# First layer of a two-layer decoder: some units of its hand-written pipeline in other slots

## The chip, the cores and the metric

The kernel runs on one core of a Trainium2 chip. Its time is the device time of one execution in microseconds (us), lower is better, given as the median of three runs. TensorE (PE) multiplies and transposes, VectorE (DVE) and ScalarE (ACT) work elementwise, GpSimd (POOL) works elementwise and issues indirect DMAs, SyncE (SP) issues the plain DMAs.

## The reference

`x` is 16 sequences of 256 tokens with 256 features. Each of two layers adds three branches to it, each on a layer norm of the running `x`:

- Layer 0: causal linear attention with 16 heads (features elu+1); cross attention with 16 heads of 16 to a context of 77 rows; a mixture of 16 experts, of which each token takes two. A token's place with its expert is a running count over all tokens before it (`ranks = cumsum(onehot)`), and a place beyond the capacity of 640 drops the token.
- Layer 1: attention over a latent, cross attention to the same context, and a gated feed-forward with quantised weights.

All arithmetic is float32.

## The kernel before, in words

`layer0` does the two attentions of layer 0 and the router, for 8 groups of 512 tokens (4 tiles of 128). `experts` then runs the 16 experts over the slots, `layer1` and the feed-forward follow. Each of these is a block that ends in a barrier over all engines.

In `layer0` the order of each engine's work is written out by hand. A loop variable `t` counts slots; `g, s = t // 8, t % 8` is a group and one of its 8 steps (lines 297 to 301). In step s of group g the engines work on several groups at once: the linear attention of group g, the preparations of groups g+1 and g+2, the output of g-1, the cross attention of g-2 and g-3, and the router of g-4. `back1` means that group g-1 exists, `ahead1` that g+1 does. From g = 8 on no new linear attention starts and the pipeline drains; the last slot is in g = 12. Engines are told apart by their own copies of the loop (SP from line 406, POOL 526, PE 785, ACT 982, DVE 1231), and each executes its list strictly in order.

PE works into eight banks. Four hold scores (L570 the linear attention's, L585 the cross attention's) and are refilled when DVE has copied them out (L1081, L1093). The other four are handed out in turn to "units", in the order of the table `UNITS` (lines 312 to 319): a unit's `room` waits until the unit four places earlier has been copied out of the same bank by ACT or DVE. So the order in the table says who waits for whom, also where no data are passed.

The units and steps that matter here:

- `turn0`, `turn1`, `turn2`: transposes of the three normalised inputs (L615). `turn1` (of g-1) feeds the queries of the cross attention, `turn0` (of g+2) the linear attention's projections.
- `proj0` (L670): the first half of the linear attention's output projection; DVE adds the residual (L1130) and so frees its bank. The residual with its bias is made by POOL (L516).
- `state0`, `state1` (L649): sums of keys times values for the next group; DVE copies them (L1156).
- `xk` (L679): the context's keys, of g-1. ACT repeats the tail of the context (`repeat_tail`, L944), then copies the keys twice (`keep_x_keys`, L935).
- `xt..` (L705, L710): transposes of the cross attention's probabilities. A tile's way to them is: scores (PE L585), mask and maximum (DVE L1093, L1097), 16 exponentials (ACT L959), sum and reciprocal (DVE L1102, L1104), product with the reciprocal (POOL L508, L509, in `normalised`), transposes (PE).
- The router: `logits`, `gate`, then `choose` on DVE (top two experts, one-hot matrix M, L1173 to L1190), `rank` (PE L774, L777), `count_ranks` (DVE L1197 to L1202), `place_tokens` (DVE L1207 to L1213), `scatter` (POOL, two times four indirect DMAs, L524), `weigh` (DVE L1219 to L1229), and two small stores of places and weights by SP (L448, L449).
- `moments`, `deviation`, `shifts`: a layer norm's statistics on DVE, the reciprocal root on POOL (L488), the shift on DVE (L1146); ACT then normalises (L979).
- `context_unit` (L141, L151, L160): work for layer 1, put into the slots of the drain.

After the last slot SP waits for all scatters and for one of the context units (`xv4`), loads the first expert's slots (L1376), and waits for its stores. SP's own order puts the stores of the last group's places and weights ahead of that load:

```
if k == 1 and there(g - 5):
    s.wait_ge(q.slots_ready, g - 4)
    ...                                   # two stores (L448, L449)
...
s.wait_ge(scattered, 16 * TOPK * NT * NG)
wait_later_made(s, "xv", 4)
load_first_slots(s, c, dr)
s.wait_ge(q.x2_stored, 16 * NG)
s.wait_ge(q.stored, 32 * NG)
```

Of the kernel before, what the change touches and what calls it, by code (L numbers as in the profile page):

```python
# [23 lines left out]
NG = B * S // T  # L24
# [153 lines left out]
def layer0(nc, ctx, c, io, dr):  # L178

    st = ExitStack()  # L180
    with st:
# [114 lines left out]

        FIRST, LAST = -2 * NS + 2, (NG + 4) * NS + 2
        WARM = 44
# [10 lines left out]
        def turned(j):  # L309
            return tuple(f"xt{j}_{n}" for n in range(NTURN))  # L310

        UNITS = {0: (("k0", 1), ("k1", 1), ("tok2", -1), ("tok3", -1), ("xq1", -2), ("xval0", -3)),
                 1: (("val0", 0),) + tuple((n, -3) for n in turned(2)) + (("col1", -1), ("xk", -1), ("v0", 1)),
                 2: (("xproj0", -3), ("proj1", -1), ("pkt", 1)),
                 3: (("val1", 0),) + tuple((n, -3) for n in turned(3)) + (("turn2a", -4), ("turn2b", -4), ("v1", 1)),
                 4: (("tok0", 0), ("tok1", 0), ("q0", 1), ("q1", 1), ("xval1", -3), ("logits", -4)),
                 5: (("val2", 0),) + tuple((n, -2) for n in turned(0)) + (("col0", 0), ("xproj1", -3), ("gate", -4)),
                 6: (("proj0", 0), ("turn1a", -1), ("turn1b", -1), ("turn0a", 2), ("turn0b", 2),
                     ("rank", -4), ("state0", 1), ("state1", 1)),
                 7: (("val3", 0),) + tuple((n, -2) for n in turned(1)) + (("xq0", -1), ("xvm", -1), ("xvl", -1))}  # L320
        place, used, front, turn_of = {}, [0, 0, 0, 0], {}, 0
# [61 lines left out]
        with nc.Block(no_gpsimd_drain=True) as block:  # L383
# [74 lines left out]
            def _(g_):  # L458
# [69 lines left out]
                for t in range(FIRST, LAST):  # L528
                    g, s = group_step(t)
                    if s == 3 and there(g + 2):  # L530
                        deviation(0, g + 2)
                        if g + 2 == 0:
                            clear_rooms()
                    if s == 1 and there(g - 3):
                        normalised(g - 3, 3)
                    if s % 2 and s > 1 and there(g - 2):
                        normalised(g - 2, s // 2 - 1)
                    if s in (0, 1) and there(g - 5):
                        scatter(g - 5, s)
                    if s == 2 and there(g + 1):  # L540
                        one_of_two(g + 1)
                    if s == 4 and there(g - 1):
                        deviation(1, g - 1)
                    if s == 5 and there(g):
                        add_bias(g)
                    if s == 7 and there(g - 3):
                        deviation(2, g - 3)
# [3 lines left out]
            def _(p):  # L551
# [230 lines left out]
                for t in range(FIRST, LAST):  # L782
# [26 lines left out]
                    if s == 1:  # L809
                        if back3:  # L810
                            x_turn(g - 3, 2)
                        if back1:
                            wait_kept(p, "tok2", g - 1)
                            wait_kept(p, "tok3", g - 1)
                            to_columns("col1", g - 1, at, 1)
                        if back1:
                            x_keys(g - 1)
                        if ahead1:
# [10 lines left out]
                    if s == 3:  # L829
                        if back3:  # L830
                            x_turn(g - 3, 3)
                        if back4:
                            turn_norm(2, g - 4, h2[(g - 4) % 2])
                        if ahead1:
                            v_rows(g + 1, 1)
                    if s == 4:
                        if now:
# [11 lines left out]
                    if s == 5:  # L849
# [9 lines left out]
                        if back4:  # L859
                            gate(g - 4)  # L860
                    if s == 6:
                        if now:
                            wait_kept(p, "col0", g)
                            project("proj0", g, aT, wo, 0)
                        if back1:
                            turn_norm(1, g - 1, h1)
                        if ahead2:
                            turn_norm(0, g + 2, h0)
                        if back4:
                            ranks(g - 4)  # L870
                        if ahead1:
                            states(g + 1, 0)
                            states(g + 1, 1)
                    if s == 7:
# [6 lines left out]
                        if back1:  # L881
                            x_rows_v(g - 1)
                    for name, j in later_at(t):
                        context_unit(name, j)
# [3 lines left out]
            def _(a):  # L888
# [92 lines left out]
                for t in range(FIRST, LAST):  # L981
# [19 lines left out]
                    if s == 1:  # L1001
                        if back3:
                            by_key(g - 3, 2)
                        if back1:
                            keep_columns("col1", g - 1, aT, 1)
                            repeat_tail(g - 1)
                            keep_x_keys(g - 1)
                        if ahead1:
# [4 lines left out]
                    if s == 3:  # L1013
# [4 lines left out]
                        if ahead1:  # L1018
                            keep_v(g + 1, 1)
                    if s == 4:  # L1020
                        if ahead2:
# [38 lines left out]
            def _(v):  # L1060
# [170 lines left out]
                for t in range(FIRST, LAST):  # L1231
# [9 lines left out]
                    if s % 2 and s > 1 and back2:  # L1241
                        sums(g - 2, s // 2 - 1)
                    if s == 1 and there(g - 5):
                        weigh(g - 5)
# [41 lines left out]
                    if s == 6:  # L1286
# [3 lines left out]
                        if back3:  # L1290
                            wait_kept(v, "xproj0", g - 3)
                            wait_kept(v, "xproj1", g - 3)
                            moments(2, g - 3, x2)
                        if back4:
                            count_ranks(g - 4)
                        if ahead1:
                            keep_state(g + 1, 0)
                            keep_state(g + 1, 1)
                    if s == 7:
                        if back1:  # L1300
                            keep_x_tail(g - 1)
                        if back3:
                            shifts(2, g - 3)
                        if back4:
                            place_tokens(g - 4)
                    for name, j in later_at(t):
                        if name == "vo":
# [1721 lines left out]
```

## Time and profile before

| | us |
|---|---|
| runs | 1669.12, 1663.44, 1670.83; median 1669.12 |
| profiled execution, its own time | 1666.73 |
| its span in the trace | 1664.7 |
| PE busy | 1514.0 (91%) |
| DVE busy | 1014.5 (61%) |
| ACT busy | 900.2 (54%) |
| POOL busy | 473.1 (28%) |

The first layer's pipeline takes the first 596 us of the span, the experts go on to about 900. In the trace a group of 8 steps takes 57 to 62 us while the pipeline is full: step 0 of g = 4 begins at 209.9, of g = 5 at 271.2, of g = 6 at 332.8. Then g = 8 begins at 446, g = 9 at 487, g = 10 at 524, and the drain ends at 591.

A timeline row reads: start, duration, engine, line, operation, out<-in, shape, count; in brackets the idle time of the engine just before it and what ended it. A duration over several instructions (x4) is from the first's start to the last's end.

### The profile page before, as it was taken

How to read it: one execution, taken by the hardware profiler on the slowest of the kernel's cores; microseconds unless marked ns; L12 is line 12 of the kernel's file. 1: busy time of each engine (PE TensorE's matmuls, PEld its weight loads, DVE VectorE, ACT ScalarE, POOL GpSimd, SP SyncE). 2: the span in 40 equal slices, each digit the busy share in tenths (PEclk: the TensorE clock that was granted, in tenths of full speed). 3: DMA queues.
4: the chain of work that ended last, by engine and by line, in shares of the span. 5: the costliest groups of instructions: out<-in, count | busy, mean ns of one | idle time of the engine just before them, and what ended most of it. 6: DMA issues, size and time to landing. Idle time of an engine off the chain costs nothing. (4 is left out here: it accounts for less than half of the span.)

```text
span 1664.7 us, 26844 instructions
## 1 busy us (share of the span) xinstructions
PE 1514.0 (91%) x9735; PEld 1071.9 (64%) x9735; DVE 1014.5 (61%) x2312; ACT 900.2 (54%) x2289; POOL 473.1 (28%) x625
## 2 busy tenths in 40 slices
PE   8999999898977889999999899999999989996299
PEld 5766777676656767787777566666666654442288
DVE  3657878888886335222222566766664568777883
ACT  4457786675786222211212555666656633597980
POOL 3212334344345300000002665555533300032100
PEclk9999999999997899999999999999999979998599
DMA  4441111111241144333424211110100000000031
GB/s 120 153 160 25 39 38 40 37 51 51 82 133 45 58 154 136 123 114 125 152 90 137 71 39 52 41 35 28 39 14 14 1 26 1 0 0 18 21 101 64
DMA packets 105281, 109.33 MB, mean 66 GB/s; under 512 B 29762, under 2 KB 94156, under 8 KB 105152
## 3 DMA queue, kind: packets, MB, share of 16 engines
q1 hardware_dynamic: 99008, 91.06, 17.8%
q0 software_dynamic: 6144, 16.57, 3.1%
q8 instruction: 79, 1.29, 0.3%
q14 instruction: 50, 0.41, 0.1%
HBM read 65.81 MB, written 42.01 MB: 65 GB/s over the span
## 5 line engine op out<-in xcount | busy, mean ns | idle before, releaser
L2121 ACT ACTIVATE c_pr<-bank,c_nmax 128x256 f32<-128x256 f32 x256 | 117.7, 472 | 118.0 <-DVE c_nmax L2238 117.9
L1827 POOL TENSOR_SCALAR c_pr<-c_pr,c_rsum 128x256 f32<-128x256 f32 x256 | 127.6, 514 | 186.4 <-DVE c_rsum L2243 186.0
L1558 ACT ACTIVATE b_G<-bank 128x320 f32<-128x320 f32 x128 | 55.9, 437 | 210.4 <-PE bank L1507 210.4
L1507 PE MATMUL bank<-b_XT,shared 128*128 128x320 f32 x512 | 154.2, 436 | 0.0
L2238 DVE TENSOR_REDUCE c_nmax<-bank 128x2 f32<-128x512 f32 x128 | 82.4, 686 | 105.8 <-PE bank L1886 102.5
L1521 PE MATMUL bank<-shared,b_G 128*128 128x256 f32 x640 | 142.2, 379 | 0.0
L959 ACT ACTIVATE a_L<-a_L,a_Lm 128x77 f32<-128x77 f32 x512 | 131.2, 353 | 4.4 <-DVE a_Lm L1097 4.3
L1521 PEld LDWEIGHTS bank<-shared,b_G 128*128 128x128 f32 x640 | 120.9, 190 | 17.8
L508 POOL TENSOR_TENSOR a_Pm<-a_L,a_xrden 128x1024 f32<-128x1024 f32 x32 | 61.3, 1916 | 220.6 <-DVE a_xrden L1104 220.6
L1507 PEld LDWEIGHTS bank<-b_XT,shared 128*128 128x128 f32 x512 | 92.2, 192 | 27.4 <-issue 1.0
L1577 DVE COPY b_Y<-bank 128x256 f32<-128x256 f32 x80 | 34.0, 425 | 119.8 <-PE bank L1521 119.6
L1569 DVE COPY b_XT<-bank 128x256 f32<-128x256 f32 x80 | 34.0, 425 | 99.9 <-PE bank L1494 99.9
L1081 DVE TENSOR_TENSOR hT_all<-bank,a_causal 128x512 f32<-128x512 f32 x128 | 79.4, 682 | 24.3 <-PE bank L570 24.1
L1786 POOL MEMSET c_minus<- 128x4 f32 x1 | 0.1, 101 | 314.8 <-POOLq L54 314.8
L2682 PE MATMUL bank<-wdT,d_raw 128*128 128x256 f32 x384 | 83.1, 379 | 0.9 <-DVE d_raw L2929 0.9
L2625 PE MATMUL bank<-hT_all,wgT 128*128 128x512 f32 x192 | 83.6, 598 | 0.0
L1897 PE MATMUL bank<-ident,c_pr 128*128 128x128 f32 x512 | 72.0, 280 | 12.4 <-POOL c_pr L1827 9.9
L2625 PE MATMUL bank<-hT_all,wuT 128*128 128x512 f32 x192 | 82.9, 593 | 0.0
L2682 PEld LDWEIGHTS bank<-wdT,d_raw 128*128 128x128 f32 x384 | 72.9, 190 | 11.0 <-DVE d_raw L2929 1.1
L1897 PEld LDWEIGHTS bank<-ident,c_pr 128*128 128x128 f32 x512 | 54.6, 140 | 37.4 <-POOL c_pr L1827 25.6
L1886 PE MATMUL bank<-c_latT,c_qT 64*128 64x256 f32 x512 | 74.5, 403 | 0.6 <-ACT c_qT L2109 0.4
L524 POOL DMA_INDIRECT t_slots_in<-a_h,a_slot_s x64 | 63.4, 990 | 35.4 <-DVE a_slot_s L1213 17.2
(386 smaller groups left out, 3433.1 us busy)
## 6 DMA issues: line engine op xcount, KB each, us to landing
shared<-L_ffn_w SPq DMA_DIRECT2D x32, 512.0 KB, 6.1
t_slots_in<-a_h SPq DMA_DIRECT2D x20, 512.0 KB, 6.2
shared<-t_slots_in SPq DMA_DIRECT2D x15, 640.0 KB, 7.0
t_slots_out<-b_Y SPq DMA_DIRECT2D x15, 640.0 KB, 4.1
hT_all<-x SPq DMA_DIRECT2D x8, 512.0 KB, 3.8
a_xr<-x SPq DMA_DIRECT2D x8, 512.0 KB, 3.9
t_x_a<-a_x SPq DMA_DIRECT2D x8, 512.0 KB, 2.9
shared<-t_x_a SPq DMA_DIRECT2D x8, 512.0 KB
```

The lines of the kernel that those rows point to most:

```text
L524: p.indirect_dma_start(out=dr["slots_in"], out_offset=bass.IndirectOffsetOnAxis(ap=slot_s[:, k, j:j + 1], axis=0), in_=h2[i % 2][:, j, :], ...
L959: x = a.activation(L[n % 2][:, h, :], L[n % 2][:, h, :], ACT.Exp, bias=Lm[n % 2][:, h:h + 1])
L1081: v.tensor_tensor(A[:, rg, :, :, :].rearrange("p e k t -> p (e k) t"), P[rg][:, :].rearrange("p (n t) -> p n t", t=128), bcast(causal[:, : ...
L1507: t = p.matmul(P[2 + n % 2][:, 0:HC], w1[e % 3][:, u, 128 * f:128 * f + 128], XT[e % 2][:, u, HC * m:HC * m + HC], start=(u == 0), stop=(u ...
L1521: t = p.matmul(P[4 + n % 3][:, 0:D], G[e % 2][:, f, 128 * j:128 * j + 128], w2[e % 3][:, f, :], start=(f == 0), stop=(f == 3))
L1827: p.tensor_scalar(pr[k][:, e, u, :], pr[k][:, e, u, :], rsum[k][:, e, u:u + 1], 1.0, ALU.mult, ALU.mult).then_inc(q.pr_ready, 1)
L1886: x = p.matmul(P[e][:, S * u:S * u + S], qT[g % 2][r, m, S * b + 128 * u:S * b + 128 * u + 128], latT[g % 2][r, S * b:S * b + S], start=Tr ...
L1897: x = p.transpose(P[2 + e][:, S * k + 128 * u:S * k + 128 * u + 128], pr[t % 2][:, e, u, 128 * k:128 * k + 128], ident)
L2121: a.activation(pr[t % 2][:, e, u, :], P[e][:, S * u:S * u + S], ACT.Exp, bias=nmax[t % 2][:, e, u:u + 1], accum_out=sums[t % 2][:, e, u:u ...
L2238: v.tensor_reduce(nmax[t % 2][:, e, :], P[e][:, :].rearrange("p (u k) -> p u k", u=2), AX.X, ALU.max, negate=True).then_inc(q.nmax_ready, 1)
L2625: t = p.matmul(bank[:, :], wT[:, u, 128 * f:128 * f + 128], hT[:, u, T * g:T * g + T], start=(u == 0), stop=(u == 1))
L2682: t = p.matmul(P[n % 8][:, 0:D], raw[:, f, T * g + 128 * j:T * g + 128 * j + 128], wdT[:, f, :], start=(f == 0), stop=(f == FC - 1))
```

## The change

- The units `rank` go from step 6 to the end of step 7, on PE and in DVE's copy of them (`count_ranks` now stands after `shifts(2)`, just ahead of `place_tokens`).
- The units `xk` go from step 1 to the end of step 3, on PE and on ACT (with `repeat_tail`, now behind `keep_v(g+1, 1)` and ahead of the exponentials of that step).
- The two halves of `scatter` go from steps 0 and 1 to steps 1 and 2. In step 1 POOL's list has `normalised(g-3, 3)` ahead of the scatter, in step 2 the scatter ahead of `one_of_two`. The loop gets one slot more.
- In step 6 `turn1` stands ahead of `proj0`.
- `weigh` of the last group is done right after its `place_tokens` (slot 95) instead of in slot 97; on DVE it so comes ahead of the three last context outputs (`vo3` to `vo5`, L1309). All other groups keep their place.
- By the table's order the banks are handed to other units: the second half of `turn0` now has the bank of `turn1`'s first half ahead of it, not that of `proj0`; `state1` has that of `proj0`.

```diff
-        FIRST, LAST = -2 * NS + 2, (NG + 4) * NS + 2
+        FIRST, LAST = -2 * NS + 2, (NG + 4) * NS + 3
...
-                 1: (("val0", 0),) + tuple((n, -3) for n in turned(2)) + (("col1", -1), ("xk", -1), ("v0", 1)),
+                 1: (("val0", 0),) + tuple((n, -3) for n in turned(2)) + (("col1", -1), ("v0", 1)),
...
-                 3: (("val1", 0),) + tuple((n, -3) for n in turned(3)) + (("turn2a", -4), ("turn2b", -4), ("v1", 1)),
+                 3: (("val1", 0),) + tuple((n, -3) for n in turned(3)) + (("turn2a", -4), ("turn2b", -4), ("v1", 1), ("xk", -1)),
...
-                 6: (("proj0", 0), ("turn1a", -1), ("turn1b", -1), ("turn0a", 2), ("turn0b", 2),
-                     ("rank", -4), ("state0", 1), ("state1", 1)),
-                 7: (("val3", 0),) + tuple((n, -2) for n in turned(1)) + (("xq0", -1), ("xvm", -1), ("xvl", -1))}
+                 6: (("turn1a", -1), ("turn1b", -1), ("proj0", 0), ("turn0a", 2), ("turn0b", 2), ("state0", 1), ("state1", 1)),
+                 7: (("val3", 0),) + tuple((n, -2) for n in turned(1)) + (("xq0", -1), ("xvm", -1), ("xvl", -1), ("rank", -4))}
...
-                    if s in (0, 1) and there(g - 5):
-                        scatter(g - 5, s)
+                    if s in (1, 2) and there(g - 5):
+                        scatter(g - 5, s - 1)
...
-                    if s == 1 and there(g - 5):
+                    if s == 1 and there(g - 5) and g - 5 < NG - 1:
                         weigh(g - 5)
...
                         if back4:
+                            count_ranks(g - 4)
                             place_tokens(g - 4)
+                            if g - 4 == NG - 1:
+                                weigh(g - 4)
```

PE's and ACT's lists of steps 1, 3, 6 and 7 are changed in the same way as the table.

## Rows read from the trace of the kernel before

**Rows 1.** The page, part 1: busy us, share of the span, instructions.

```profile
PE 1514.0 (91%) x9735; PEld 1071.9 (64%) x9735; DVE 1014.5 (61%) x2312; ACT 900.2 (54%) x2289; POOL 473.1 (28%) x625
```

**Rows 2.** The waits of PE in 0 to 640: us in total, times, longest.

```profile
PE bank L774 <- DVE a_M L1190: 13.2, 5, 4.6
PE bank L705 <- POOL a_Pl L509: 12.5, 4, 4.7
PE bank L615 <- DVE a_x L1130: 9.3, 5, 3.3
```

**Rows 3.** Timeline of DVE in steps 6 and 7 of g = 4.

```profile
259.21 0.68 DVE L1130 TENSOR_TENSOR a_x<-bank,a_xr 128x512 f32<-128x512 f32 x1
...
261.73 0.22 DVE L1197 TENSOR_TENSOR a_rank<-bank,a_carry 128x64 f32<-128x64 f32 x1
...
263.03 0.92 DVE L1156 TENSOR_TENSOR hT_all<-bank,a_headsel 128x136 f32<-128x136 f32 x4
...
268.71 0.25 DVE L1104 RECIPROCAL a_xrden<-a_xrden 128x16 f32<-128x16 f32 x1
...
272.47 0.16 DVE L1146 SCALAR_TENSOR_TENSOR a_shift<-a_mean_var,a_rstd 128x4 f32<-128x4 f32 x1 [0.39 <-POOL a_rstd L488]
...
273.56 2.48 DVE L1081 TENSOR_TENSOR hT_all<-bank,a_causal 128x512 f32<-128x512 f32 x4
```

**Rows 4.** Timeline of POOL in step 7 of g = 4.

```profile
269.05 1.92 POOL L508 TENSOR_TENSOR a_Pm<-a_L,a_xrden 128x1024 f32<-128x1024 f32 x1 [12.24 <-DVE a_xrden L1104]
...
271.43 1.01 POOL L488 TENSOR_TENSOR a_rstd<-a_var_eps,a_minus 128x4 f32<-128x4 f32 x1
```

**Rows 5.** Timeline of PE: step 6 of g = 1, 2 and 3, and step 0 of g = 5.

```profile
90.26 1.99 PE L670 MATMUL bank<-a_wo,wdT 128*128 128x256 f32 x8 [1.98 <-ACT wdT L894]
...
143.72 0.65 PE L615 MATMUL bank<-ident,hT_all 128*128 128x128 f32 x4 [1.24 <-DVE a_x L1130]
...
200.44 0.66 PE L615 MATMUL bank<-ident,hT_all 128*128 128x128 f32 x4 [1.50 <-DVE a_x L1130]
...
276.73 1.98 PE L622 MATMUL bank<-a_hT,a_xwq 128*128 128x512 f32 x4
```

**Rows 6.** Timeline of ACT in step 1 of g = 5: the context's tail and keys.

```profile
285.37 0.58 ACT L944 ACTIVATE a_ctxl<-a_ctxT 128x416 f32<-128x416 f32 x1
285.82 0.95 ACT L935 ACTIVATE a_xkm<-bank,a_parity 128x308 f32<-128x308 f32 x2
```

**Rows 7.** Timeline of POOL in g = 8, 9 and 10: scatters and products.

```profile
465.76 0.98 POOL L524 DMA_INDIRECT t_slots_in<-a_h,a_slot_s  x1 [0.31 <-issue]
468.76 1.91 POOL L508 TENSOR_TENSOR a_Pm<-a_L,a_xrden 128x1024 f32<-128x1024 f32 x1 [2.02 <-DVE a_xrden L1104]
...
507.00 1.91 POOL L508 TENSOR_TENSOR a_Pm<-a_L,a_xrden 128x1024 f32<-128x1024 f32 x1 [1.41 <-DVE a_xrden L1104]
...
530.43 1.07 POOL L524 DMA_INDIRECT t_slots_in<-a_h,a_slot_s  x1 [1.88 <-DVE a_slot_s L1213]
...
535.33 1.93 POOL L508 TENSOR_TENSOR a_Pm<-a_L,a_xrden 128x1024 f32<-128x1024 f32 x1
```

**Rows 8.** Timeline of DVE in g = 9 and 10: a small sum, a reciprocal.

```profile
497.52 2.59 DVE L1221 TENSOR_TENSOR a_psum<-a_prob 128x4 f32<-128x4 f32 x1
...
531.14 0.25 DVE L1104 RECIPROCAL a_xrden<-a_xrden 128x16 f32<-128x16 f32 x1
```

**Rows 9.** Timelines of the layer's end: POOL, DVE, SP and PE in turn.

```profile
584.22 0.97 POOL L524 DMA_INDIRECT t_slots_in<-a_h,a_slot_s  x1 [0.30 <-issue]
...
589.81 0.16 DVE L1219 TENSOR_SCALAR a_prob<-a_prob 128x8 f32<-128x8 f32 x1
...
592.55 2.27 SPq L1376 DMA_DIRECT2D shared<-t_slots_in  x5
...
589.00 2.35 PE L175 MATMUL bank<-ident 128*128 128x128 f32 x20
596.04 1.08 PE L1494 MATMUL bank<-ident,shared 128*128 128x128 f32 x4 [4.69 <-PEq L54]
```

More of the change, by code:

```diff
@@ L815, in _ @@
                             to_columns("col1", g - 1, at, 1)
-                        if back1:
-                            x_keys(g - 1)
                         if ahead1:
@@ L835, in _ @@
                             v_rows(g + 1, 1)
+                        if back1:
+                            x_keys(g - 1)
                     if s == 4:
@@ L861, in _ @@
                     if s == 6:
+                        if back1:
+                            turn_norm(1, g - 1, h1)
                         if now:
@@ L864, in _ @@
                             project("proj0", g, aT, wo, 0)
-                        if back1:
-                            turn_norm(1, g - 1, h1)
                         if ahead2:
                             turn_norm(0, g + 2, h0)
-                        if back4:
-                            ranks(g - 4)
                         if ahead1:
@@ L882, in _ @@
                             x_rows_v(g - 1)
+                        if back4:
+                            ranks(g - 4)
                     for name, j in later_at(t):
@@ L1005, in _ @@
                             keep_columns("col1", g - 1, aT, 1)
-                            repeat_tail(g - 1)
-                            keep_x_keys(g - 1)
                         if ahead1:
@@ L1019, in _ @@
                             keep_v(g + 1, 1)
+                        if back1:
+                            repeat_tail(g - 1)
+                            keep_x_keys(g - 1)
                     if s == 4:
@@ L1293, in _ @@
                             moments(2, g - 3, x2)
-                        if back4:
-                            count_ranks(g - 4)
                         if ahead1:
```

## The prediction

> **What bounds the kernel now.** The page comes first: PE is busy 91% of the span [rows 1], so a PE wait removed looks like time gained. The list of PE's waits over the first 640 us has three that the change touches [rows 2]: 13.2 us in five ranks that wait for DVE's matrix M, 12.5 us in four transposes that wait for POOL's product, 9.3 us in five `turn0` that wait for DVE's residual add. Then the timelines of each engine, group by group, to see whether PE is what the group waits for. In the full pipeline it is not. From 281.5 (first masks of step 1) to 321.5 (the add of `proj0`) of g = 5 DVE has next to no idle time, and the same holds in g = 4 and 6. From the add on the chain stays on DVE and POOL [rows 3, 4]: add 259.21, moments and `count_ranks`, sums done at 268.96, POOL's product from 269.05 and its root until 272.44, DVE's shift at 272.47, places, masks of the next group at 273.56. These masks, then the copy of `k0`, release PE's query product at 276.73 [rows 5]. PE's wait in step 6 is recovered slack. In g = 1 to 3 there is no router and PE is the bound more often. In the drain (g = 8 to 11) the bound is the chain of one tile: sums, product on POOL, transposes. The layer's end is set by SP [rows 9].
>
> **Turn1 ahead of proj0.** Nothing is added; PE waits at another place. In g = 1 PE stands 1.98 us before `proj0` [rows 5]; `turn1`'s input is there some 1.2 us earlier, so its eight transposes (0.9 us on PE) move into the wait: -0.9. In g = 2 the second `turn0` waits 1.24 us for the add (until 143.72). Now it, half a microsecond, and `state0`, another half, run before that moment and only `state1` waits: -1.0. In g = 3 the same wait is 1.50 (until 200.44) and gives PE 1.1, of which the copy of `k0` passes on 0.9 (DVE was idle 0.81 us there, for ACT). From g = 4 on PE is 2 us earlier at the end of step 6, and DVE and POOL are not: 0. Sum -2.8; the bounds are 0 and -9.3, the whole row [rows 2].
>
> **Ranks to the end of step 7.** PE no longer stops for M, DVE no longer counts before the scores. `count_ranks` is 1.30 us (261.73 to 263.03) [rows 3]. Without it the sums are ready 1.3 us earlier, POOL starts and ends 1.3 us earlier (its 3.4 us are unchanged [rows 4]), the shift is at 271.2, then come the 1.3 us of counting and the places: masks at 273.6, as before. What would hide it, a count inside the 3.4 us in which DVE waits for POOL, is not used, since it stands behind the shift. The same in g = 5 to 9. In g = 10 the count stood inside that wait, so the scatter of group 6 starts 1.3 us later; nothing waits for it. Term 0, bounds -3 (half a microsecond a group, if PE's lead is of use) and +3 (as much, if a bank is now waited for: `tok3` in g = 5 and 6, `xval0` later have the bank of the ranks).
>
> **Context keys to the end of step 3.** On PE the 1.1 us only change place. On DVE the masks of step 1 waited 2.45 us for PE in g = 3 and 4, so they start 1.1 us earlier, but the copies of `q0` are released by ACT. There the move costs: tail and keys, 0.58 and 0.95 us, 1.4 together [rows 6], leave a step with slack and come just ahead of the 16 exponentials, and the keys must wait until PE has made them, behind `v1`. By my reading ACT is later by 0.5 us in g = 4, 0.3 of it on the path in g = 5 (DVE has 0.76 us of slack), 0 in g = 6 (no norm ahead), 1.5 in g = 7, where the keep of the values then holds the column transposes, `xproj1` and the choice. Sum +2.3; bounds -2 (the 1.1 us of g = 3 and 4 pass on) and +7 (1.4 us in each of g = 3 to 7).
>
> **Scatters.** Each half is 4.9 us on POOL (530.43 to 535.33) [rows 7]. The move past the products cuts both ways. For: in g = 10 the last tile's sums are ready at 531.39 [rows 8], and POOL, busy with the first half, makes the product at 535.33: -3.9, all on the chain, for PE was idle 4.27 us there and then works without a gap until 557. Against: both halves now stand back to back ahead of the next product. In g = 8 the product of step 1 ends at 461.8, the two halves fill 461.9 to 471.9, and the product that began at 468.76 begins at 472.0: +3.2; behind it are the root for which DVE already waited 1.52 us, and the transposes for which PE waited 2.51. In g = 9: product from 497.3 (0.9 earlier), halves until 509.8, next product at 509.9 for 507.00: +2.9. Queued behind it are DVE's third masks and PE's transposes, which both waited for just this. In g = 5 to 7 the next product has 3 to 4 us of slack: root and product are 0.8 to 2.0 us late, off the path by 0.1 in g = 5, 0 else. Net +2.2. One more effect: PE ran the first 5 us after the wait of g = 10 at half the granted clock, 1.97 us for eight transposes that otherwise take 1.09; without that wait I take half of the 2.9 us that this cost, -1.5; bounds 0 and -3.
>
> The trace has DVE's small sum (L1221) at 2.59 us while POOL multiplies [rows 8] and at 0.16 in g = 10, where POOL was scattering. After the change POOL multiplies there too. The Trainium skill (SBUF — State Buffer, section "SBUF: two separate sides") says that a DVE operation with two SBUF inputs and a GpSimd one that reads SBUF lock each other out for whole instructions, with which the 2.59 agrees; by it DVE's weights of g = 10 end about 2 us later. The sum is the same by either, for what stands behind them, the add of `xproj0`, has over 2 us of slack.
>
> **The last weights.** Now DVE waits for the last context output and weighs at 589.81; SP stores the places, loads the first slots from 592.55 to 594.82, and the next block's first transposes are at 596.04, 1.2 us on [rows 9]. After: `weigh` (1.8 us) at 574.5, in 4 us of DVE idle time, stores at once; the load waits for the last scatter (issued until 585.2) and lands before 591. Late next is PE's filler, which ends at 591.35; with the same 1.2 us the block begins at 592.6: -3.5. Bounds -1 (the barrier costs more behind PE) and -4.7 (the whole idle row).
>
> **Sum.** -2.8 + 0 + 2.3 + 2.2 - 1.5 - 3.5 = -3.3. The profiled execution took 1666.73 (span 1664.7 and 2.0 around it), which gives 1663.4. It lies 2.4 under the median of the runs, so the median after would be 1665.8 by that; I take 1665.
>
> **The rivals.** (1) PE is the bound after all: the waits for M and for the add, 13.2 + 9.3 [rows 2], go and stay gone, with the -3.5 of the end: 1669 - 26 = 1643, or, with half of them, 1654. For it: 91% busy. Against: PE's product at 276.73 waits for a DVE chain that has no idle time but POOL's. (2) Slower: POOL's double block, 9.9 us, is the bound in every group from g = 5, not only in g = 8 and 9. It decides when the next product's sums are ready less than 10.2 us after the product of step 1 ends; in g = 5 that distance is 11.8, in g = 8 and 9 it is 7.0. If DVE's and PE's order shifts so that it falls to 9 in g = 5 to 7, each adds 1 to 2 us; with the keys at +7 and the clock at 0 the total is -2.8 + 7 + 2.2 + 4 - 3.5 = +7, and if DVE's longer waits bring PE's half clock into two more groups (+3 each), +13: 1682. (3) The change does nothing: the gains of the end are eaten by the same landing of the scatters, and the drain's two sides cancel: 1669.
>
> **How the numbers follow.** Forecast 0.55, with its own range 1659 to 1671; (1) 0.2; (2) 0.13; (3) 0.12. A measurement here can tell about 0.5% (8 us) from no change: faster means under 1660.8, slower over 1677.5. Faster: rival 1 and an eighth of the forecast, 0.27. Slower: most of rival 2, 0.1. Within: 0.63. The range 1653 to 1674 leaves out the full form of (1) and the far end of (2).
>
> **What would show it.** Right: no `turn0` waits for the add; PE waits instead at the query product of step 0 and at the masks; the groups 4 to 7 keep 60 us; POOL's product in g = 8 and 9 has no idle time before it and starts 3 us later against the group, in g = 10 it follows the sums at once; the first expert's transposes begin 1.2 us after PE's filler. Wrong: a group in the full pipeline shortened by over 1 us, PE's idle time in 100 to 450 falling as much as the span, or the load of the first slots still the last thing before the barrier.

## The result: slower by 0.8%, and the trace after

| | before | after |
|---|---|---|
| runs, us | 1663.4 to 1670.8, five | 1675.0 to 1685.7, five |
| median | 1667.9 | 1681.6 |
| ratio of the runs | 1 | 1.008 (95%: 1.005 to 1.011) |
| profiled execution, its own time / span | 1666.7 / 1664.7 | 1675.0 / 1673.1 |

The forecast was 1665 with 1653 to 1674 as its range: 17 us off, with the wrong sign. The profiled execution of after is the fastest of its five, so its trace shows 8 us of the 14.

In the kernel after, the lines of `layer0` quoted here are lower by one than before for all engines but DVE (PE L705 is L704, POOL L524 is L523); DVE's L1081 to L1229 keep their numbers, the next block's are higher by one. PE's busy time is the same to 0.2% [rows 1].

```profile
PE 1517.5 (91%) x9735; PEld 1071.8 (64%) x9735; DVE 1016.4 (61%) x2312; ACT 900.6 (54%) x2289; POOL 473.1 (28%) x625
```

The waits of PE in 0 to 640 us of after (columns as in [rows 2]):

```profile
PE bank L704 <- POOL a_Pl L508: 10.8, 7, 3.8
PE bank L614 <- ACT a_oT L911: 9.1, 3, 3.7
PE bank L648 <- DVE a_x L1130: 5.9, 4, 2.5
PE bank L584 <- issue: 4.5, 6, 1.1
PE bank L704 <- issue: 3.1, 5, 0.9
PE bank L773 <- DVE a_M L1190: 2.6, 1, 2.6
```

Of the three waits of [rows 2] the one for M has fallen from 13.2 to 2.6 and that of `turn0` for the add (9.3) has become 5.9 of the sums for the add (L648). Two other kinds stand high now: PE waits for ACT's copy of the values (L911), and PE waits for "issue", that is for nothing that the trace shows.

To see where the time went, take the start of the same instruction in both traces, here and there along the span. The table gives the differences to before in us, one profiled execution a column: the starts of `masks` (L1081, to g = 7) and `masked` (L1093, g = 8 and 9), of the slots (L1213) and of the next block's first transposes (L1494). Executions differ by up to 2.6 us already at the first row, so read how a column changes:

| start in before | after | scatters_alone | scatters_unsent | pool_pow_instead | scatters_back | halves_apart | paced_scatters | six_and_two | twos_at_four_steps |
|---|---|---|---|---|---|---|---|---|---|
| 47.8 (g = 0) | -1.0 | -0.7 | -2.6 | +1.8 | +0.2 | +2.2 | -0.9 | -1.1 | +0.2 |
| 289.7 (g = 5, step 2) | -4.0 | +2.2 | -5.6 | -1.2 | -2.7 | -0.8 | -2.1 | -4.1 | -1.1 |
| 302.5 (g = 5, step 4) | +2.9 | +7.5 | +1.2 | +0.1 | -2.7 | -1.2 | +4.2 | -0.8 | -1.0 |
| 351.3 (g = 6, step 2) | +4.9 | +9.5 | +3.3 | -0.2 | -2.0 | -0.1 | +6.1 | -1.1 | -1.3 |
| 363.4 (g = 6, step 4) | +11.2 | +15.1 | +9.6 | -1.3 | -2.6 | +0.9 | +7.1 | +1.7 | -1.3 |
| 410.6 (g = 7, step 2) | +9.1 | +13.0 | +7.5 | -3.1 | -4.7 | -2.0 | +5.2 | -1.3 | -4.2 |
| 420.9 (g = 7, step 4) | +16.2 | +18.4 | +14.0 | -2.4 | -4.7 | -1.4 | +5.6 | +2.5 | -2.9 |
| 463.9 (g = 8, step 3) | +13.5 | +16.0 | +11.4 | -4.4 | -3.0 | -0.6 | +7.0 | +1.8 | -3.1 |
| 472.3 (g = 8, step 5) | +16.7 | +19.2 | +14.6 | -2.4 | -3.0 | +4.4 | +14.2 | +5.0 | -0.6 |
| 502.2 (g = 9, step 3) | +15.9 | +19.4 | +13.7 | -3.2 | -3.0 | +3.6 | +13.3 | +4.1 | -1.5 |
| 509.4 (g = 9, step 5) | +19.7 | +23.2 | +17.6 | -0.7 | -3.0 | +3.6 | +21.2 | +5.3 | -1.5 |
| 558.5 (slots of g = 10) | +17.3 | +23.1 | +18.4 | -3.7 | -1.6 | +3.2 | +18.5 | +6.4 | -3.7 |
| 574.3 (last slots) | +16.5 | +22.6 | +17.4 | -8.6 | -2.2 | +2.5 | +18.1 | +5.9 | -4.5 |
| 596.0 (next block) | +10.5 | +21.2 | +11.8 | -15.2 | -8.2 | -3.5 | +13.2 | -0.2 | -10.5 |

After gains 3.0 us up to step 2 of g = 5. Then it loses 6.9, 6.3 and 7.1 us, each between step 2 and step 4 of g = 5, 6 and 7; 3.2 and 3.8 in g = 8 and 9; it gets back 2.4 in g = 10 and 6.0 at the layer's end. The three losses of 7 us are the whole result.

The timelines of POOL, ACT and PE in the first of them (start, duration; in brackets idle time before it and what ended it):

```profile
284.91 1.25 POOL L523 DMA_INDIRECT t_slots_in<-a_h,a_slot_s  x1 [0.18 <-issue]
...
294.13 0.97 POOL L523 DMA_INDIRECT t_slots_in<-a_h,a_slot_s  x1 [0.30 <-issue]
...
287.61 0.60 ACT L893 ACTIVATE wuT<-bank 128x512 f32<-128x512 f32 x1 [0.55 <-issue]
...
296.51 0.69 ACT L911 ACTIVATE a_oT<-bank,a_eps 128x512 f32<-128x512 f32 x1 [8.31 <-remote]
...
289.58 1.08 PE L603 MATMUL bank<-hT_all,shared 128*32 128x128 f32 x32
...
292.74 0.27 PE L704 MATMUL bank<-ident,a_Pm 128*128 128x128 f32 x1 [0.35 <-issue]
...
293.46 0.32 PE L704 MATMUL bank<-ident,a_Pm 128*128 128x128 f32 x1 [0.45 <-issue]
...
294.90 0.30 PE L709 MATMUL bank<-ident,a_Pl 128*104 128x128 f32 x1 [0.46 <-issue]
...
297.25 1.97 PE L614 MATMUL bank<-ident,a_h 128*128 128x128 f32 x8 [2.05 <-ACT a_oT L911]
```

POOL issues eight scatters without a break, 284.9 to 295.1. By the code ACT has nothing to wait for from 290.7 on (the values are made at 289.58 + 1.08), yet it does nothing until 296.5, 1.4 us behind the last scatter. From 292 on PE makes one transpose about every 0.72 us instead of one every 0.14, and is busy for 1.53 of the 4 us to 296. When both are released the granted clock is near its lower level (0.56 of full speed in 296 to 300), and the eight transposes take 1.97 us for 1.09. ACT then has the values, the probabilities, the columns, the context's tail and its keys to catch up with, ahead of the 16 exponentials. ACT stands in the same way at 358.7 to 367.0 and 419.3 to 430.5. Of its 8.3, 8.3 and 11.1 idle us, 5.8, 5.7 and 4.2 lie behind the end of the matmuls that it waits for. I call this a hold-up, and an unbroken run of scatters a train.

What is late is PE's signal. The trace records when each semaphore rises, and a wait is put down to "remote" when its semaphore rose over 1.5 us after the last instruction that raises it had ended. PE's values (L603) end at 290.66 and their semaphore rises at 296.49, just ahead of ACT's start; the semaphores of PE's work that ended at 291.25, 293.78 and 295.20 follow within 0.16 us. Such a semaphore I call a late signal. In the first 600 us of all seventeen traces, every wait of over 0.6 us that a signal late by over 0.5 us ended was one of ACT, DVE or POOL for PE (189 waits), and every such signal came inside a train of scatters or less than 2.2 us behind it; the one kernel without scatters, pool_pow_instead below, has none. The ends of matmuls are modelled in the trace, so it does not tell whether PE's results are late or only the signal.

### The profile page after: what moved, and what is told of

Read it like the earlier page. It is cut to its first block and busy times, and to the rows that moved or that the text cites. A ratio compares the mean times of both kernels' runs of the same rounds, so it can differ in the third digit from the quotient of the medians.

```text
span 1673.1 us, 26843 instructions
## 1 busy us (share of the span) xinstructions
PE 1517.5 (91%) x9735; PEld 1071.8 (64%) x9735; DVE 1016.4 (61%) x2312; ACT 900.6 (54%) x2289; POOL 473.1 (28%) x625
## 3 DMA queue, kind: packets, MB, share of 16 engines
q1 hardware_dynamic: 99008, 91.06, 17.6%
## 5 line engine op out<-in xcount | busy, mean ns | idle before, releaser
L1081 DVE TENSOR_TENSOR hT_all<-bank,a_causal 128x512 f32<-128x512 f32 x128 | 79.4, 682 | 40.0 <-PE bank L569 39.8
L523 POOL DMA_INDIRECT t_slots_in<-a_h,a_slot_s x64 | 63.2, 987 | 26.3 <-issue 17.8
```

Of the source, the lines that this page charges most:

```text
L523: p.indirect_dma_start(out=dr["slots_in"], out_offset=bass.IndirectOffsetOnAxis(ap=slot_s[:, k, j:j + 1], axis=0), in_=h2[i % 2][:, j, :], ...
L1081: v.tensor_tensor(A[:, rg, :, :, :].rearrange("p e k t -> p (e k) t"), P[rg][:, :].rearrange("p (n t) -> p n t", t=128), bcast(causal[:, : ...
```

## The experiments

Each ran beside the kernel before on the same chip; the ratio is to it, with its 95% interval. Three theories go by letters: T, a train of eight scatters holds up PE and ACT; P, the loss is only that products and roots stand behind the scatters in POOL's list; K, the later context keys are the loss. Some of the expectations say row for train.

**scatters_back**: the one part undone.

```
-                    if s in (1, 2) and there(g - 5):
-                        scatter(g - 5, s - 1)
+                    if s in (0, 1) and there(g - 5):
+                        scatter(g - 5, s)
```

> The changed kernel with the two scatter halves back at steps 0 and 1, ahead of the products of probabilities; all its other parts stay. Theory T (eight scatters in one unbroken row of 10.2 us hold up PE and ACT from about their sixth microsecond on): the three losses of 7 us in g = 5, 6 and 7 and those of 3.2 and 3.8 us in g = 8 and 9 go, the -2.4 of g = 10 too; what is left is the gain up to step 3 of g = 5 (-4.5), the keys and the end (-6 to -3): 4 to 9 us under the kernel before, 1659 to 1664. Rival P (the loss is only POOL's order: products and roots that stand behind the scatters): the same sum here. Rival K (the context keys, ACT's tail and keys just ahead of the exponentials, are the 7 us): the slowdown stays, 1676 to 1685.

Measured: 1661.1 against 1671.7, ratio 0.994 (0.992 to 0.996). K falls. What is left of the change makes the kernel faster.

**scatters_alone**: the same lines changed in the kernel before, with its last slot one later.

> The kernel before with one edit: the scatter halves at steps 1 and 2 behind the products. T and P: 3 x 7 + 3.2 + 3.8 - 2.4 = 25.6 us over the kernel before, less what slack takes back, so 1682 to 1694. K: within 4 us of the kernel before, 1664 to 1672.

Measured: 1687.7, ratio 1.009 (1.006 to 1.013). The column shows +5.3, +5.6, +5.4, +3.2 and +3.8 where the hold-ups and late products are. One part makes the whole loss; T and P are still level.

**halves_apart**: the halves behind the products of steps 1 and 3.

```
-                    if s in (1, 2) and there(g - 5):
-                        scatter(g - 5, s - 1)
+                    if s in (1, 3) and there(g - 5):
+                        scatter(g - 5, s // 2)
```

> The changed kernel with the halves behind the products of two different steps, 1 and 3, so that no train is longer than 4.9 us. T: no stall of PE or ACT in g = 5 to 7 and no 10 us block, so 1658 to 1666. P: the second half now delays the root of step 4 (the product of step 3 is ahead of it) and the first the pair of step 2, and the products of g = 8 and 9 are still late by one half at a time: 1670 to 1680.

Measured: 1662.4, ratio 0.994 (0.993 to 0.996). With trains of 4.9 us the losses of 7 us are gone; ACT's copy in g = 5 waits for its bank alone:

```profile
294.24 0.69 ACT L911 ACTIVATE a_oT<-bank,a_eps 128x512 f32<-128x512 f32 x1 [2.84 <-PE bank L603]
```

T holds. In g = 8 the kernel still loses 5.0 us between steps 3 and 5 (the table's -0.6 and +4.4); I have not followed that one.

**scatters_unsent**: the rows are not sent.

```
-  bounds_check=SLOTS - 1, oob_is_err=False)
+  bounds_check=SLOTS - 1 if i == NG - 1 else 0, oob_is_err=False)
```

> The changed kernel; the scatters of groups 0 to 10 have a bound of 0, so that almost no row is written (the slots of these groups stay zero), while POOL runs the same eight instructions in a row at the same place; the last group's are whole. T in the form that the transfers are what holds up PE and ACT: the stalls of g = 5 to 7 vanish, the POOL order costs of g = 8 and 9 stay: 21 us less than the changed kernel, 1658 to 1664. T in the form that the making of descriptors by POOL is what does it, and P: as the changed kernel, 1677 to 1685.

Measured: 1681.8, ratio 1.007 (1.004 to 1.010), all losses as in after. POOL's DMA queue moved 0.01 MB beside the train of g = 5 (282 to 298) where in after it moved 1.05, and the hold-up is the same:

```profile
q0 software_dynamic: 384, 0.01, 1.6%
...
295.07 0.69 ACT L911 ACTIVATE a_oT<-bank,a_eps 128x512 f32<-128x512 f32 x1 [8.50 <-remote]
```

So it is not the transfers of the rows. The Trainium skill (Perfetto Trace Analysis, section "DMA Instruction — SWDGE (GPSIMD)") says that the profiler's interval of such an instruction is the time in which GpSimd's cores write descriptors, not that of the data. The trace agrees: 0.97 us each with the rows sent or not.

**pool_pow_instead**: POOL as busy, without scatters.

```
-  p.indirect_dma_start(...).then_inc(scattered, 16)
+  if i or k or j:
+      p.wait_ge(scattered, 16 * (2 * NT * i + NT * k + j))
+  p.tensor_tensor(idle[:, :], eid[:, 1:5], minus[:, :], ALU.pow).then_inc(scattered, 16)
```

> The changed kernel with each scatter replaced by a POOL power of 128x4 (1.0 us, as L487 in the profile), so that POOL is busy for about as long at the same place and issues no indirect DMA; the slots stay zero. Theory T (the scatter instruction itself, not the rows it sends and not POOL's being busy, holds up PE and ACT): no stall in g = 5 to 7; the late products of g = 8 and 9 stay. 21 us under the changed kernel (1681.6): 1656 to 1665. Rival P (POOL's order alone): as the changed kernel, 1677 to 1685, with the same steps of +7 between masks.

Measured: 1646.1, ratio 0.985 (0.983 to 0.987). POOL is taken for 9.07 us in a row and holds up nobody; ACT waits for PE's bank, and PE makes the eight transposes in 1.09 us. POOL, ACT and PE in turn:

```profile
287.48 9.07 POOL L526 TENSOR_TENSOR a_idle<-a_eid,a_minus 128x4 f32<-128x4 f32 x8
...
293.53 0.69 ACT L912 ACTIVATE a_oT<-bank,a_eps 128x512 f32<-128x512 f32 x1 [2.53 <-PE bank L604]
...
293.39 1.09 PE L705 MATMUL bank<-ident,a_Pm 128*128 128x128 f32 x8
```

P falls for g = 5 to 7: its price there is 1.3 us in g = 5, none in g = 6 and 0.7 in g = 7. It stands for g = 8 and 9: +2.0 and +2.5. And the whole is 24 us faster than before, 14 us more than the other edits bring: before pays for its scatters as well. Set against scatters_back, each from its own first line, 8.6 us of the 14 stand at the table's last line, 4.3 of them between the last two lines of slots, where before has a train of eight (559.4 to 569.4) beside which DVE's choice of experts waits 8.9 us (scatters_back has one too, and ACT waits 5.0 us behind it). The rest of the 14 stands behind the first layer, where no scatter runs, or in the difference between executions; I can't place it.

**rows_halved**: the scatters take 64 partitions.

```
-  ap=slot_s[:, k, j:j + 1], ...  in_=h2[i % 2][:, j, :]
+  ap=slot_s[0:64, k, j:j + 1], ...  in_=h2[i % 2][0:64, j, :]
```

> The changed kernel, each scatter for 64 of the 128 partitions (half of the rows stay out of the slots): as many instructions in a row, half as many descriptors. If the hold-up comes from the number of descriptors in the train: it begins only near the train's end or not at all in g = 5 to 7, 1657 to 1670. If it comes from the instructions in a row: as the changed kernel, 1676 to 1685, unless each is much shorter on POOL.

Measured: 1679.0, ratio 1.007 (1.004 to 1.010). The train is 9.7 us for 10.2, and ACT's waits are the same:

```profile
294.85 0.69 ACT L911 ACTIVATE a_oT<-bank,a_eps 128x512 f32<-128x512 f32 x1 [8.36 <-remote]
...
426.27 0.69 ACT L911 ACTIVATE a_oT<-bank,a_eps 128x512 f32<-128x512 f32 x1 [11.13 <-remote]
```

The number of rows sent does not matter either.

**pair_between_halves**: the pair of masked keys between the halves.

```
+                    if s == 1 and there(g - 5):
+                        scatter(g - 5, 0)
                     if s == 2 and there(g + 1):
                         one_of_two(g + 1)
+                    if s == 2 and there(g - 5):
+                        scatter(g - 5, 1)
```

> The changed kernel with the pair of masked keys (2.7 us on POOL) between the two scatter halves instead of behind them. If a pause of 2.7 us is enough to end the hold-up: no PE or ACT stall of over 2 us in g = 5 to 7, the keys are ready 5 us earlier and the product of step 3 is as late as now: 1660 to 1667. If what counts is the number of scatters in 13 us and not their being unbroken: stalls stay at 5 to 7 us a group, 1678 to 1686.

Measured: 1670.7, ratio 1.000 (0.999 to 1.002), between the two ranges. It decides by a thing that I had overlooked: in g = 7 there is no next group, so no pair, and the train is unbroken again. In g = 5 and 6, with the pair, masks of step 4 are late by 2.2 and 1.7 us; in g = 7, without it, by 7.0 (+1.3 to +8.3), and ACT stood for 11.2 us:

```profile
422.69 0.69 ACT L913 ACTIVATE a_oT<-bank,a_eps 128x512 f32<-128x512 f32 x1 [11.21 <-remote]
```

**paced_scatters**: a power of 1 us behind every second scatter.

```
+                        if j % 2 and i < NG - 1:
+                            ...
+                            p.tensor_tensor(idle[:, :], eid[:, 1:5], minus[:, :], ALU.pow).then_inc(c.idle_s, 1)
```

> The changed kernel with a POOL power of 128x4 (about 1.0 us) behind every second scatter of groups 0 to 10, so that POOL spends 14 us on the eight scatters in four rows of two. If an unbroken row is what holds PE and ACT up: hold-ups of 8 us vanish in g = 5 to 7, while the 4 us more on POOL delay products and roots by up to 4 us in each of g = 5 to 9: 1668 to 1682. If the number of scatters in a stretch counts: hold-ups stay and the pauses come on top, 1688 to 1702.

Measured: 1681.0, ratio 1.006 (1.004 to 1.009), as slow as after for another reason. POOL spends 286.8 to 301.1 on the eight; ACT's copy is late by 1.1 us only, and the first large wait is that of DVE's shift, which waits for a root that POOL has behind the train. ACT and DVE:

```profile
293.66 0.69 ACT L918 ACTIVATE a_oT<-bank,a_eps 128x512 f32<-128x512 f32 x1 [3.56 <-PE bank L610]
...
304.84 1.88 DVE L1153 SCALAR_TENSOR_TENSOR a_shift<-a_mean_var,a_rstd 128x4 f32<-128x4 f32 x1 [5.13 <-POOL a_rstd L489]
```

Beside the pairs of this run no engine waits for "remote", and PE at most 0.6 us for "issue". The hold-up is cut short and not gone: PE's signal for the values still comes 1.1, 0.9 and 0.9 us after their end in g = 5 to 7, where after has 5.8, 5.7 and 4.2. So the break is what counts, and one other POOL instruction of 1.05 us behind every second scatter takes away most of it. P is real where POOL is taken for 14 us: +6.3 in g = 5, +7.2 and +7.9 in g = 8 and 9.

**six_and_two**: six behind the product of step 1, two behind that of step 3.

```
+                    if s == 1 and there(g - 5):
+                        scatter(g - 5, 0, range(NT))
+                        scatter(g - 5, 1, (0, 1))
+                    if s == 3 and there(g - 5):
+                        scatter(g - 5, 1, (2, 3))
```

> The changed kernel with six scatters in a row behind the product of step 1 (7.5 us) and two behind that of step 3. If the hold-up ends with the row (as in the traces so far, some 1.5 us behind it), it is 2.5 us shorter a group than with eight: the masks of step 4 of g = 5 to 7 are late by 3 to 5 us each instead of 7: 1668 to 1676. If six are as harmless as four: 1660 to 1666. If as bad as eight: 1677 to 1683.

Measured: 1667.6, ratio 0.999 (0.997 to 1.000). Groups 5 to 7 lose 3.3, 2.8 and 3.8 us, about half of what they lose with eight. Not all of it is the six. PE's signal comes 3.2 us late behind the six in g = 5, but only 1.3 and 1.5 in g = 6 and 7, and in g = 5 and 7 the two scatters of step 3 hold up DVE's masks as well. POOL and DVE in g = 5:

```profile
300.17 0.98 POOL L523 DMA_INDIRECT t_slots_in<-a_h,a_slot_s  x1 [0.30 <-issue]
...
301.70 2.48 DVE L1084 TENSOR_TENSOR hT_all<-bank,a_causal 128x512 f32<-128x512 f32 x4 [3.05 <-remote]
```

DVE waits for PE's scores and transposes, which end at 299.56 and 300.14; both signals come at 301.6 to 301.7, 0.5 us behind the pair. So even a train of two holds an engine up where that engine needs PE just then. A hold-up ends soon behind its train, 0.5 us behind this pair and 1.4 us behind after's eight, and so can grow with the train's length.

**twos_at_four_steps** and **twos_never_touching**: toward a better kernel. Both have the other edits but the keys as before; the second puts step 2's two scatters behind the pair of keys.

```
-                    if s in (0, 1) and there(g - 5):
-                        scatter(g - 5, s)
+                    if s < 4 and there(g - 5):
+                        scatter(g - 5, s // 2, (2 * (s % 2), 2 * (s % 2) + 1))
```

> keys_and_scatters_back (1657.7) with the eight scatters of a group in four pairs, at steps 0 to 3 (2.2 us each). Theory T (the length of the unbroken train counts): the short hold-ups that trains of four still have (DVE, PE and ACT for 1 to 4 us near 400, 450 and 465 us in the traces) go, and in g = 10 the product waits for half as long: 4 to 8 us less, 1649 to 1655. Rival: trains of four cost nothing, and each scatter that moves behind a product delays the drain: 1657 to 1662.

> twos_at_four_steps (1652.9) with the third pair behind the masked keys of step 2, so that in the full pipeline no row is longer than two. If rows of four (steps 1 and 2 there) still cost: 1647 to 1652. If not, or if the keys' place costs as much: 1651 to 1656.

Measured: 1652.9, ratio 0.991 (0.988 to 0.994), and 1661.5, ratio 0.994 (0.992 to 0.996). The first has the lowest median of the kernels that do the whole work, 1% under before; but its interval overlaps that of keys_and_scatters_back (0.990 to 0.994, next), so what the four pairs themselves bring is not settled. The second lies above both of its ranges. Between the two nothing is settled either: their profiled spans are 1652.0 and 1652.4, and the latter is that of the fastest of its seven executions. In the second, with no train over two in g = 5 and 6, ACT is still held up there, 0.5 us behind a pair that ends at 290.98 (and again at 354.3):

```profile
291.51 0.69 ACT L913 ACTIVATE a_oT<-bank,a_eps 128x512 f32<-128x512 f32 x1 [3.68 <-remote]
```

In the full pipeline of the first POOL's trains are two or four, and PE is never idle in 284 to 300:

```profile
292.00:296.00 4.00, 4.00 (x66) 3.47 (x59) 3.93 (x14) 2.02 (x5) 3.98 (x6) 1.00 0.67 192
```

(columns: stretch, its length, busy us and instructions of PE, its weight loads, DVE, ACT and POOL, granted clock, DMA share, GB/s). The same stretch in after, DMA nearly as busy, with ACT at nothing:

```profile
292.00:296.00 4.00, 1.53 (x6) 0.55 (x5) 3.93 (x7) 0.00 (x0) 3.36 (x5) 1.00 0.66 246
```

**The other parts alone.** Their edits are those of the change's diff, each by itself in the kernel before; keys_and_scatters_back has the turn, the ranks and the last weights together.

> The kernel before with three of the five edits: norm's turn first, ranks at the end of step 7, last weights at once; context keys and scatters stand as before. If the later keys cost 2.3 us as predicted: 2 us faster than scatters_back (1661.1), so 1656 to 1661. If they cost nothing or gain: 1661 to 1665. The masks of g = 7, 8 against those of g = 3 show it within one execution.

Measured: 1657.7, ratio 0.992 (0.990 to 0.994), against 0.994 (0.992 to 0.996) with the keys late. The order of the two is the expected one, the intervals overlap. In the traces, each from its own first row, the kernel with late keys is 1.0 to 1.2 us behind at most masks of g = 6 and up to step 2 of g = 7, and level at step 2 of g = 5; further on short hold-ups at trains of four cover it.

> The kernel before with the last group's weights behind its places (step 7) and nothing else. Predicted term -3.5: the load of the first slots then waits for the last scatter instead of the stores, PE's filler is late next, the block starts 3.5 us earlier against the last slots (574.3): 1668 and 1671 become 1664 to 1668. Rival: the landing of the scatters or the filler gives it back, less than 1 us.

Measured: 1668.4 against 1670.4, ratio 0.999 (0.998 to 1.000): the runs gain 2.0 us. In the trace it is 17.1 us from the last slots to the next block (578.43 to 595.54) where before has 21.7. SP, PE and the block's first transposes:

```profile
590.66 2.22 SPq L1378 DMA_DIRECT2D shared<-t_slots_in  x5
...
592.20 2.35 PE L175 MATMUL bank<-ident 128*128 128x128 f32 x20
595.54 0.63 PE L1496 MATMUL bank<-ident,shared 128*128 128x128 f32 x4 [1.00 <-PEq L54]
```

> The kernel before with norm's turn ahead of proj0 in step 6 and nothing else. Predicted term -2.8, all of it by the masks of g = 4; then level. 1665 to 1669 against 1670; if PE's waits of the full pipeline were the bound it would be -9, 1659 to 1663.

Measured: 1656.9 against 1669.7, ratio 0.993 (0.991 to 0.995). Its trace agrees with the term: masks of g = 4 are 2.5 us earlier than at its start, the next block 2.8. Its runs say 12.8 us, 8 to 15 by the interval: more than the term, and more than the 9 us of the other case. The two traces do not show that gain, for the profiled execution of before is 3.0 us under the median of 1669.7 and that of turn_alone, 1662.3, is the slowest of its five, 5.4 over theirs. So what the edit is worth in a usual execution, and where, stays open.

> The kernel before with the ranks' product and their counting at the end of step 7 and nothing else. Predicted term 0 (-3 to +3): masks of g = 5 to 9 within 0.5 us of the kernel before, the slots of each group 1.3 us nearer to the masks that follow; the last slots about 1.3 us later. 1668 to 1673.

Measured: 1667.0 against 1669.7, ratio 0.999 (0.998 to 1.001): no difference.

## Why the prediction was wrong, step by step

**What bounds the kernel**: right for the ranks. M's wait on PE went from 13.2 to 2.6 us in after [rows 2] and to 2.9 in ranks_alone, and no time came of it. Rival (1), 1643 or 1654, is out for the change as a whole. It is not out for PE's waits for the add: turn_alone's runs gained more than that whole row (9.3).

**Turn1 ahead of proj0, -2.8**: held in the traces, -2.5 to -3.0 by the masks of g = 4 and 5; too small by turn_alone's runs (-12.8). The parts but the scatters were forecast at -4.0 together (-2.8 + 0 + 2.3 - 3.5), and scatters_back, which has just these, measured -10.6 (7 to 14). The second `turn0`, which waited for the add in g = 2 and 3 [rows 5], waits no more in g = 3, and the second sum behind it waits 0.30 instead (in g = 2 it still waits 1.17, now for ACT's copy of the first, and the sum 0.56):

```profile
195.65 1.04 PE L614 MATMUL bank<-ident,hT_all 128*128 128x128 f32 x8
196.52 0.63 PE L648 MATMUL bank<-shared,wuT 128*128 128x136 f32 x4
197.45 0.70 PE L648 MATMUL bank<-shared,wuT 128*128 128x136 f32 x4 [0.30 <-DVE a_x L1130]
```

**Ranks, 0**: right. **Context keys, +2.3**: right in sign by the traces, but only 1.0 to 1.2 us, from the end of g = 5 on and not in g = 4; the runs do not settle it. Its own parts on the path add up to 1.8 (0.3 and 1.5); the 2.3 counts the 0.5 of g = 4 besides its 0.3.

**Scatters, +2.2 and -1.5**: the step that failed, at its sentence on g = 5 to 7: "root and product are 0.8 to 2.0 us late, off the path by 0.1 in g = 5, 0 else." What POOL's order costs there was indeed small (1.3, 0 and 0.7 with pool_pow_instead). What I left out, with no term for it, is that a train of scatters holds up engines that wait for nothing from it. The three groups lost 20.3 us in place of 0.1 (16.3 in scatters_alone, with all other units in their old places). By the runs the move of the scatters cost 20 us (1681.6 for scatters_back's 1661.1), where the two terms add up to +0.7. The pieces in the drain were close. The late products of g = 8 and 9 cost 3.2 and 3.8 for 3.2 and 2.9; they begin at the end of the train, as forecast:

```profile
485.49 1.94 POOL L507 TENSOR_TENSOR a_Pm<-a_L,a_xrden 128x1024 f32<-128x1024 f32 x1
...
526.63 1.95 POOL L507 TENSOR_TENSOR a_Pm<-a_L,a_xrden 128x1024 f32<-128x1024 f32 x1
```

In g = 10 the product follows its sums at once [rows 7, 8], and the transposes behind it run at full clock, 1.09 us for eight, as the -1.5 had it; but the low clock now stands behind the three hold-ups (0.56 in 296 to 300, 0.50 in 366 to 370 and in 430 to 434). DVE, POOL and PE:

```profile
550.83 0.25 DVE L1104 RECIPROCAL a_xrden<-a_xrden 128x16 f32<-128x16 f32 x1
551.38 1.72 DVE L1221 TENSOR_TENSOR a_psum<-a_prob 128x4 f32<-128x4 f32 x1
...
551.16 1.91 POOL L507 TENSOR_TENSOR a_Pm<-a_L,a_xrden 128x1024 f32<-128x1024 f32 x1 [4.24 <-DVE a_prob L1219]
...
553.63 1.09 PE L704 MATMUL bank<-ident,a_Pm 128*128 128x128 f32 x8 [1.36 <-POOL a_Pl L508]
```

Without hold-ups that is worth 3.8 us (pool_pow_instead, -3.8 from +0.1 to -3.7; forecast 3.9); in after 2.4 is left, because the eight scatters that follow hold up ACT from 558.6 to 563.7. The small sum L1221 took 1.72 us for 0.16 as POOL multiplies beside it, as the prediction had from the Trainium skill (SBUF — State Buffer, section "SBUF: two separate sides"), and nothing waited for it.

The profile had shown the effect, and I read past it. Before has PE idle for "issue" at 401 and 454, and DVE waiting for "remote" at 402, 454 and 569, each inside a train or just behind one. PE and DVE, behind a train of four that ends at 401.5:

```profile
402.22 0.64 PE L604 MATMUL bank<-hT_all,shared 128*32 128x128 f32 x11 [1.00 <-issue]
...
402.39 1.63 DVE L1093 TENSOR_TENSOR a_L<-bank,a_amask 128x308 f32<-128x308 f32 x4 [2.87 <-remote]
```

The idle times that the trace gives to no releaser were the ones to ask about before making a train twice as long.

**The last weights, -3.5**: the gain is there, -4.6 by the trace of weights_alone (its bound was -4.7; the runs say -2.0) and -6.0 in the whole change, where the last slots also come later against PE's context units. In weights_alone what is late next is what was named, PE's filler, which ends at 594.55, 1.0 us before the block. In after it is not. The filler ends at 604.65, but SP's load, 1.4 us behind the last scatter (issued until 601.7), ends at 605.27, and the block begins 1.2 us after that, as in before. The load is still the last thing before the barrier, which the prediction had among its signs of being wrong. SP's stores and load, then PE [rows 9]:

```profile
593.17 0.32 SPq L447 DMA_DIRECT2D t_slot_g<-a_slot_g  x1
...
603.05 2.22 SPq L1377 DMA_DIRECT2D shared<-t_slots_in  x5
...
602.16 2.49 PE L175 MATMUL bank<-ident 128*128 128x128 f32 x20
606.49 0.63 PE L1495 MATMUL bank<-ident,shared 128*128 128x128 f32 x4 [1.83 <-PEq L54]
```

**Rival (2)** named 1682 with a chance of 0.13, and its place (POOL's double block in every group from g = 5) was the right one; its mechanism was not. POOL's products were not what came late, and its price of 1 to 2 us a group was a quarter of the measured one. That its 1682 meets the measured 1681.6 is luck.

**Left open.** That trains of scatters make PE's signals late is shown by the runs; why they do is not. It is neither the rows' transfer nor their number nor POOL's being busy. One lead: the packets of the instruction queues (q8, 79 of 16 KB over the span, and q14, 50 of 8 KB). In five of the first six trains of after such a packet lands inside, as at 287 and 289 in the first. But they land in harmless trains of four too (291 and 292 in before) and in the same stretch of pool_pow_instead, and there is none inside after's train of 553.8 to 563.8, which held up ACT and PE, nor inside the three of before with the longest hold-ups. The Trainium skill (Runtime: NRT & Kernel Launch, section "Instruction fetch mechanics") gives blocks of 256 instructions and room for 2048 on PE; by it PE should not run dry within 10 us, which is an estimate and speaks against this reading. No run here tested it. Why a train of four costs 1 to 3 us at some places (400 and 451 in before) and nothing at most others is open as well: that an engine must need PE's signal at that moment is part of it, as six_and_two shows.

## What to carry to other kernels

A long unbroken run of indirect DMAs on GpSimd is not only GpSimd's own time. In the full pipeline here a group lost 6 to 7 us with eight in a row, about 3 with six and two, and mostly nothing with fours or pairs; but fours cost 1 to 3 us at some places, and a pair can hold an engine up for 2 us. Spread such runs, or put another GpSimd instruction between them, before asking what stands behind them in the queue, and keep them away from the moments at which another engine waits for TensorE. And idle time that a trace gives to "issue" or "remote" is a finding: look at what all other engines do in it before lengthening that thing.

## What the runs showed of the hardware

- An indirect DMA of 128 rows of 1 KB takes POOL 0.97 us and the next follows 0.30 later, with the rows sent or not; with 64 rows it takes 0.90.
- Beside trains of scatters PE's semaphores rise late: up to 5.8 us after the modelled end of the matmul in after, up to 2.1 beside a pair (twos_never_touching). In the first 600 us of all traces no late signal of another engine ended a wait, and with powers in the scatters' place (pool_pow_instead) none of PE's did.
- In the train of g = 5 in after PE executed one transpose per 0.72 us. ACT did nothing for 8.3 to 11.1 us in the three trains of the full pipeline, until 1.4 to 1.6 us behind the last scatter; DVE went on (292 to 296: 3.93 of 4 us busy).
- One POOL power of 128x4 (1.05 us) behind every second scatter brought the lateness in g = 5 to 7 from 5.8, 5.7 and 4.2 us down to 1.1, 0.9 and 0.9.
- Behind the hold-ups of g = 5 to 7 PE ran at or near the lower of its two clocks (0.56, 0.50 and 0.50 granted; it had been busy for 1.53, 1.08 and 1.46 of the 4 us before), and eight transposes took 1.97 us for 1.09.
